# Attention on TensorE: the mix of values issued ahead of the scores of the present couple

## What is computed

```python
qr = heads(sr @ Wq_r.T + bq_r)        # the same for qi, kr, ki, vr, vi
ar = einsum('bhnd,bhmd->bhnm', qr, kr) + einsum('bhnd,bhmd->bhnm', qi, ki)
ai = einsum('bhnd,bhmd->bhnm', qi, kr) - einsum('bhnd,bhmd->bhnm', qr, ki)
mag = sqrt(ar ** 2 + ai ** 2 + 1e-08) * HD ** (-0.5)
w = softmax(mag, axis=-1)
out_r = einsum('bhnm,bhmd->bhnd', w, vr)   # and out_i with vi
attn_r = out_r @ Wo_r.T + bo_r             # and attn_i with Wo_i
```

## Time and profile before

| | before |
|---|---|
| median of 3 runs | 2832.51 us (2831.17 to 2833.8) |
| the profiled execution: its own time | 2832.54 us |
| its span in the profile | 2830.7 us |
| TensorE, share of the span | 96% |
| VectorE | 74% |
| ScalarE | 44% |
| granted TensorE clock, mean | 0.98 |
| blocks 1 to 15 of the attention, scores of couple 0 to scores of couple 3 | 1455.96 to 2204.15 us from the start |

### The profile page before, as it was taken

One profiled execution on the slowest core, in us unless ns is written; L12 is line 12 of the kernel. 1 busy time (PEld: TensorE's weight loads), 2 busy tenths in 40 slices (PEclk: granted clock), 3 DMA queues, 4 the chain that ended last, 5 costly groups with the idle time before them and its releaser, 6 DMA issues. The chain is left out here.

```text
span 2830.7 us, 43833 instructions
## 1 busy us (share of the span) xinstructions
PE 2720.3 (96%) x16320; PEld 2339.1 (83%) x16320; DVE 2091.1 (74%) x3548; ACT 1235.7 (44%) x1873; POOL 152.6 (5%) x185
## 2 busy tenths in 40 slices
PE   8999999999899998999999999999999899999797
PEld 6888888888778876888889999999999777877686
DVE  5697778873567865687877877877777769999863
ACT  2222442244543336333454554444444556464643
POOL 2000000000000000010100100100000000000200
PEclk9999999999999999999999999999999899999899
DMA  6555556544755867468723223232232654445310
GB/s 244 202 187 185 187 192 220 193 160 152 240 169 185 266 233 267 135 207 287 250 81 105 60 89 89 60 97 81 69 101 68 169 129 96 104 96 133 104 34 12
DMA packets 493716, 420.41 MB, mean 149 GB/s; under 512 B 282273, under 2 KB 397089, under 8 KB 493345
## 3 DMA queue, kind: packets, MB, share of 16 engines
q1 hardware_dynamic: 459168, 341.20, 39.4%
q0 software_dynamic: 17792, 60.89, 5.7%
q10 hardware_dynamic: 16640, 16.78, 1.8%
HBM read 328.62 MB, written 90.18 MB: 148 GB/s over the span
## 5 line engine op out<-in xcount | busy, mean ns | idle before, releaser
L54 PE MATMUL banks<-a_hi 128*128 128x512 f32 x1024 | 399.8, 390 | 14.0 <-DVE a_lo L367 13.9
L55 PE MATMUL banks<-a_lo,a_hi 128*128 128x512 f32 x1024 | 399.2, 390 | 0.0
L56 PE MATMUL banks<-a_hi,a_lo 128*128 128x512 f32 x1024 | 399.1, 390 | 0.0
L54 PE MATMUL banks<-b_hi 128*128 128x512 f32 x896 | 355.8, 397 | 22.6 <-DVE b_lo L790 11.9
L55 PE MATMUL banks<-b_lo,b_hi 128*128 128x512 f32 x896 | 352.0, 393 | 0.0
L56 PE MATMUL banks<-b_hi,b_lo 128*128 128x512 f32 x896 | 351.7, 393 | 0.0
L54 PE MATMUL banks<-sx,g_hi 128*128 128x256 f32 x1024 | 294.4, 287 | 5.8 <-DMA sx<-s_scr 4.0
L55 PE MATMUL banks<-sx,g_hi 128*128 128x256 f32 x1024 | 291.4, 285 | 0.0
L56 PE MATMUL banks<-sx,g_lo 128*128 128x256 f32 x1024 | 291.3, 284 | 0.0
L1639 DVE TENSOR_SCALAR t_ks<-banks,cols 64x256 f32<-64x256 f32 x512 | 236.5, 482 | 28.9 <-PE banks L56 22.1
L54 PEld LDWEIGHTS banks<-a_hi 128*128 128x128 f32 x1024 | 192.7, 188 | 55.5 <-DVE a_lo L367 14.8
(11 more groups left out here) (202 smaller groups left out, 5517.5 us busy)
## 6 DMA issues: line engine op xcount, KB each, us to landing
w_ring<-w_first SPq DMA_DIRECT2D x192, 512.0 KB, 4.3
w_ring<-w_second SPq DMA_DIRECT2D x160, 512.0 KB, 5.0
sx<-s_scr SPq DMA_DIRECT2D x64, 512.0 KB, 4.4
a_scr<-t_at SPq DMA_DIRECT2D x256, 128.0 KB, 2.1
s_axng<-a_scr SPq DMA_DIRECT2D x64, 512.0 KB, 5.2
g_wraw<-w_pieces SPq DMA_DIRECT2D x74, 256.0 KB, 4.7
w_ring<-w_second SPq DMA_DIRECT2D x64, 256.0 KB, 5.3
c<-h_scr ACTq DMA_DIRECT2D x16, 1024.0 KB, 7.8
```

Of the source, the lines that this page charges most:

```text
L54: mm(out, ahi, bhi, start=first, stop=False, **more)
L55: mm(out, ahi, blo, start=False, stop=False, **more)
L56: return mm(out, alo, bhi, start=False, stop=last, **more)
```

## The change

In `block_body` of TensorE the two calls of each place trade places: `mix(b - 1, m - 1)` is issued ahead of `score(b, m - 1)`, and `mix(b - 1, 3)` ahead of `score(b, 3)`. The waits go with the calls. Nothing else differs; VectorE's, ScalarE's, GpSimd's and SyncE's streams are the same word for word.

```diff
                     project(b, m, 1)
-                    score(b, m - 1)
                     if not first:
                         mix(b - 1, m - 1)
+                    score(b, m - 1)
                 values(b, 0)
                 values(b, 1)
-                score(b, KD - 1)
                 if not first:
                     mix(b - 1, KD - 1)
+                score(b, KD - 1)
                 values(b, 2)
```

## The result

The changed kernel takes 2841.4 us as the median of 13 runs, against 2831.0 us for the kernel before in 13 runs beside them. The ratio is 1.0041, with a 95% interval from 1.0034 to 1.0048: 11.6 us slower (9.6 to 13.6). One of the runs before was a slow one (3040.91 us) and is left out of the ratio, which is why this is more than the 10.4 us between the two medians. The forecast was 12.8 us, and the time forecast, 2845.3, stands 3.9 us above the measured one, 1.5 us of it because the kernel before itself came out at 2831.0 here and not at 2832.5.

A forecast was written before the change was run, and what follows sets the result against it. TensorE, busy throughout the loop, bounds the kernel. A new wait of 0.87 us in 13 blocks (11.3 us) plus 1.5 us for blocks 1 and 15 gives 2832.5 + 12.8 = 2845.3 us; range 2838.5 to 2852.5, chance 0.81.

The forecast's parts named there:

- The bound: In the loop over blocks TensorE, busy 260.00 of 260.00 us, sets the time, so what delays it is paid in full.
- the sum: Prediction's total: 0.87 us in each of blocks 2 to 14 (11.3 us), 1.5 us for blocks 1 and 15, +12.8 us.
- The new wait: Couple 3's mix on TensorE waits for `o_low` of couple 2, 0.87 us for each steady block.
- the restart: TensorE, couple 3: the mix's first weight load comes 0.11 us after `o_low` ends, as in block 1.
- the last row of the mix: TensorE, couple 3: the mix's last row starts 0.88 us after its first weight load.
- The handover: Turns between kinds of matmuls on TensorE: 0.09 us surcharge once per couple before and after, sum zero, bounds -5.4 to +5.4 us.
- The wait is paid once: Rival, chance 0.09: the first 0.87 us delay gives VectorE its slack back for good; time 2833.4 us.
- A cheaper handover: Rival, chance 0.02: no wait, and 0.09 us saved at 60 places on TensorE; 5.4 us faster, 2827.1 us.
- The clock falls: Rival, chance 0.04: about 0.65 us idle per block lowers TensorE's clock, 1.7 us more each block; 2870.8 us.
- A dearer restart: Rival, chance 0.04 beyond 2852.5: TensorE restarts 0.1 to 0.4 us later in 13 blocks; with dearer turn 2855 us.
- The output projection next: Behind couple 3, the output projection needs `o_low` and has 0.9 us to spare, so it costs nothing.

## Why the prediction was right, point by point

**The bound.** TensorE was full and paid the wait in full: +0.84 us of period in the loop (0.87 in the sum). In all, the attention of the two traces differs by 12.4 us (0.75 in block 1, 13 x 0.84, 0.76 in block 15), where the sum had 12.8. The time of the runs, 11.6 us with an interval of 4 us, fits both numbers and could not have told the terms apart; the period does.

**The new wait** is where it was said to be, in each block, on `o_low` of couple 2; another bank or a shorter chain takes it away, one operation more adds to it. Its terms, in block 3: `o_low` 0.06 us late (0.05 in the sum), the restart 0.05 (0.11), the last row of the mix 0.88 behind its weight load (0.88). The restart is the only term that was clearly mis-sized. I had one row for it, from the written-out block 1, and used it for the loop, whose waits sit on other instructions. With this alone put right the sum would have given 0.81 a block; the other 0.03 us are the hundredth that `o_low` was later and the rounding of the rows, so 0.87 came so near to 0.84 partly by small errors against each other. The text gave a rival to a dearer restart and to a cheaper one only a wider lower bound, and it was cheaper.

**The handover.** The guess that it is worth zero holds within 0.02 us a block. Rows of block 3, couple 0, in the changed kernel:

```profile
1557.33 0.28 PE L56 MATMUL banks<-sx,g_lo 128*128 128x256 f32 x1
1557.33 0.31 PEld L2091 LDWEIGHTS banks<-t_ptl,t_v 128*128 128x128 f32 x2
1557.45 0.27 PE L2091 MATMUL banks<-t_ptl,t_v 128*128 128x128 f32 x1
```

The mix's first load runs during the last projection, the mix starts 0.12 us behind it, as one projection behind another, so with no surcharge, and its scores follow 0.99 us behind the start of the mix (0.97 in the text). The period with no wait, 51.84 against 51.86, is the whole effect of the swap. The stretch in which TensorE waits in neither kernel says the same: from the last projection ahead of the pair of couple 0 to the last product ahead of the pair of couple 3 there are 21.89 us before (1559.62 to 1581.51) and 21.86 now (1557.33 to 1579.19). The rule of the Trainium skill that would have made it 5.4 us dearer ("TensorE: Matmul & The Clock Gate", "Part 3: Packing small matmuls — row/col tiling") doesn't hold for this pair: the load overlaps a matmul on the same rows at this place (1557.33), and at couple 3 too where nothing holds the mix up (1582.99 in the kernel with another bank).

**The rivals.** *The wait is paid once*: no, the thirteen periods of the loop are all 52.70, and VectorE waits 0.36 us for TensorE at the start of its chain as before. *A cheaper handover*: 0.02 us a block, and the wait stands against it. *The clock falls*: the granted clock is 1.00 over the loop with 0.60 us of recorded idle time in each block. *A dearer restart*: it was cheaper. *The output projection next*: not in the changed kernel, where its weight load starts at 1587.20, as late as all else behind the mix (8.01 us behind the last product ahead of the mix, and 7.15 before); in the kernel with the pair one product later it is the bound, with 1.90 us over the 51.84 of the changed order without a wait (1.8 expected).

**Where the rest of the difference is.** The two spans differ by 9.2 us, not by 12.4. Everything ahead of block 1 took 3.9 us less in the profiled execution of the changed kernel, in code that is the same in both. The nine kernels of the experiments share this code too, but for a few instructions of block 0 in four of them, and the start of the last projection ahead of the first scores of block 1 lies anywhere from 1451 to 1458 us in their traces. So a span alone can't settle a few microseconds, and the period can.

## What to carry to other kernels

Before two neighbours on a full engine trade places, ask which of them waits for the later signal: the other one is its cover, and its length is a first estimate of what the swap can cost, per turn of the loop. Here the scores cover 0.58 us and 0.84 were lost: the rest are the handovers around them and the later `o_low`. A helper engine that is busy three quarters of the time can be without any slack in the part of the loop that decides; look for the stretch from where it last ran dry to the signal, and check whether it is anchored to the full engine, because then the wait comes back in every block. Here the loss went without a change of order, by where the result goes (another bank that happened to be free); that version ran as fast as the kernel before (0.9992, 0.9983 to 1.0002), not shown to be faster.

## What the runs showed of the hardware that I had not expected

- A wait carried by TensorE's weight load restarts it 0.05 us after VectorE's recorded end, one on an event instruction ahead of it 0.115 us after; the restart changed in block 1 with nothing but the order in which three waits are written. This is the mix's; the output projection with the pair one product later restarts 0.13 us behind `o_low` in the loop and 0.07 in block 1, and why these differ was not looked into.
- VectorE operations of 64 x 256 that read PSUM are recorded with 0.48 us and start as little as 0.40 apart. Adding one to a full chain cost 0.39 and 0.40 us.
- A weight load of 128 columns runs ahead under a matmul on the same rows, while the load of 32 columns behind it waits for the turn, about 0.09 us, whether a projection or a mix stands ahead of it.
